# A two-layer token tower: each half of the tokens as one chain, experts group by group, gate rows by DMA

## The reference, cut to what matters

```python
h = embed(tokens, pp)                                 # table rows through one linear map
# layer 0
x = layernorm(h); k, q = tanh(gelu(x@W1+b1)@W2+b2)    # keys and queries, 64 phases each
ret = causal(cos/sin(q) . cos/sin(k)) @ (x@Wv)        # per sequence, divided by position
h = h + x + layernorm(ret)@Wo + bo
h = moe(h, experts=8, top_k=2, hidden=256, gelu)      # operand normalised per expert
# layer 1
x = four blocks of (linear attention, 8 heads; feed forward 64 -> 256 -> 64, gelu)
h = h + ...; h = moe(h, experts=8, top_k=2, hidden=256, relu)
```

## Time and profile before

| what | value |
|---|---|
| median of 3 runs | 662.95 us (662.91 to 663.2) |
| profiled execution | 665.71 us, its span 664.0 us |
| PE busy | 564.1 us (85% of the span) |
| DVE busy | 423.9 us (64%) |
| ACT busy | 405.1 us (61%) |
| granted TensorE clock, mean | 0.928 of full |
| DMA moved | 11.03 MB |

### The profile page before, as it was taken

How to read it: one execution, slowest core, us unless ns; L and a number is a source line. 1 busy time by engine, 2 the same in 40 slices (tenths; PEclk the granted TensorE clock), 3 DMA queues, 4 the chain that set the end, 5 groups by cost and what they waited for, 6 DMA issues and landing times.

```text
span 664.0 us, 8277 instructions
## 1 busy us (share of the span) xinstructions
PE 564.1 (85%) x2840; PEld 294.7 (44%) x2862; DVE 423.9 (64%) x1105; ACT 405.1 (61%) x674; POOL 24.0 (4%) x36
## 2 busy tenths in 40 slices
PE   0679793599899999867999999999864998999995
PEld 0345783434333333355676666766523333333331
DVE  6779579645333453588899999999866254333333
ACT  0458231286576676424978878888741666766773
POOL 8060000000000000000000000000000000000000
PEclk9979796799899999896999999999986899999998
DMA  7901000000000000300000000000000000001001
GB/s 209 219 1 36 13 1 0 1 0 1 0 1 0 1 0 1 95 1 0 1 1 1 1 2 1 0 1 1 1 0 1 0 1 0 1 1 32 1 0 32
DMA packets 16343, 11.03 MB, mean 17 GB/s; under 512 B 10064, under 2 KB 15216, under 8 KB 16240
## 3 DMA queue, kind: packets, MB, share of 16 engines
q1 hardware_dynamic: 14000, 9.93, 6.0%
q10 hardware_dynamic: 2304, 0.58, 0.5%
HBM read 9.47 MB, written 1.05 MB: 16 GB/s over the span
## 4 chain that ended last, share of the span: by engine, by line
PE 54%; DVE 32%; issue 6%; ACT 4%; DMA 3%; SPq 1%; DVEq 0%; ACTq 0%
PE bank L1521 20%; PE bank L1537 18%; DVE l1mom L1204 3%; DVE Xs L1197 3%; DMA w1m<-in_w1e 3%; PE bank L1526 2%; PE bank L1328 2%; DVE Xn L1229 2%; PE bank L1394 2%; DVE mom L831 1%; DVE small L1165 1%; DVE Cen L1210 1%; PE bank L1385 1%; DVE Mm L1190 1%; DVE Ph L1159 1%
## 5 line engine op out<-in xcount | busy, mean ns | idle before, releaser
L652 ACT ACTIVATE Hd<-bank,b1all 128x512 f32<-128x512 f32 x256 | 155.5, 690 | 74.2 <-PE bank L1521 74.2
L1537 PE MATMUL bank<-Hd,w2m 128*64 128x512 f32 x512 | 123.1, 604 | 5.0 <-issue 5.0
L1060 DVE SCALAR_TENSOR_TENSOR Tmp<-bank,b2col,Wb 128x512 f32<-128x512 f32 x56 | 42.0, 751 | 130.6 <-PE bank L1537 130.6
L1521 PE MATMUL bank<-Ph,w1m 64*128 64x512 f32 x256 | 69.0, 644 | 3.6 <-ACT Hd L652 2.1
L1521 PE MATMUL bank<-XT,w1m 64*128 64x512 f32 x256 | 67.6, 638 | 3.9 <-ACT CT L636 1.7
L1537 PEld LDWEIGHTS bank<-Hd,w2m 128*64 128x64 f32 x512 | 31.5, 136 | 52.3 <-issue 51.5
L712 ACT ACTIVATE Hd<-bank,lvecs 128x512 f32<-128x512 f32 x64 | 38.9, 688 | 5.7 <-PE bank L1658 5.5
L1521 PEld LDWEIGHTS bank<-Ph,w1m 64*128 64x128 f32 x256 | 24.8, 193 | 38.6 <-ACT Hd L652 19.3
L1521 PEld LDWEIGHTS bank<-XT,w1m 64*128 64x128 f32 x256 | 23.9, 193 | 40.3 <-ACT Hd L652 21.6
L1064 DVE TENSOR_TENSOR Rest<-Rest,Tmp 128x512 f32<-128x512 f32 x56 | 38.8, 692 | 1.9
L1609 PEld LDWEIGHTS bank<-bd,XT 128*128 128x128 f32 x256 | 32.8, 200 | 16.1 <-ACT Hd L712 15.0
(11 more groups left out here) (220 smaller groups left out, 911.8 us busy)
## 6 DMA issues: line engine op xcount, KB each, us to landing
Ph<-in_x SPq DMA_DIRECT2D x4, 512.0 KB, 9.2
Ph<-in_itok SPq DMA_DIRECT2D x4, 384.0 KB, 9.9
w1m<-in_w1e SPq DMA_DIRECT2D x1, 1028.0 KB, 18.6
w2m<-in_w2e SPq DMA_DIRECT2D x2, 512.0 KB, 13.7
w1m<-in_w1e SPq DMA_DIRECT2D x1, 1024.0 KB, 5.7
out<-Hs SPq DMA_DIRECT2D x16, 64.0 KB, 1.7
Hd<-in_w1all SPq DMA_DIRECT2D x1, 512.0 KB, 14.9
bd<-in_l_attn SPq DMA_DIRECT2D x8, 64.0 KB, 4.6
```

The lines of the kernel that those rows point to most:

```text
L652: ac.activation(Hd[:, st.ring, k // 2, k % 2, :], bank[k][:, :], func, bias=b1all[:, m, st.e, k // 2:k // 2 + 1]).then_inc(up_read, 1)
L1060: ve.scalar_tensor_tensor(dst, bank[4 + st.ring][:, :], b2, Wb[:, st.ring, :], ALU.add, ALU.mult).then_inc(down_read, 1)
L1521: te.matmul(bank[k][:, :], w1m[hs, st.e, k // 2 * P:(k // 2 + 1) * P], operand[hs, gslice(st.g)], start=True, stop=True).then_inc(up_made, 1)
L1537: ins = te.matmul(bank[4 + st.ring][h * D:(h + 1) * D, :], w2m[:, st.e, hc * D:(hc + 1) * D], Hd[:, st.ring, hc, h, :], start=(hc == 0), s ...
```

## The change

The names of bank plan, step order and lists all change, but what is computed stays, except that the phases are reduced by another formula and gates stay float32.

- **Half by half.** PE, ACT and DVE take half 0 through scores, retrieval, norms, projection, operand and gates as early as their lists let them, with pieces of half 1 between. `norm_retrieved(1)` is behind half 0's gates, and half 1's projection, norms and operand run beside the first 16 steps.
- **Phases in two passes** instead of three (scale and offset go into the sine's own scale and bias); ACT's sines stand between gelus and tanhs of other groups.
- **Steps group by group.** Step n has group n // 8 and expert n % 8; each group is turned back and normed while the next ones run. The norm before layer 1 is per group for groups 2 and 3.
- **Gates by transfers.** The 16 gate rows of a group are turned in float32, copied to `CT` (now `[16, 2048]`), written to a DRAM scratch (`spill`), and per step two DMAs from there broadcast one row each over 64 partitions of `Wb` (`spread`), which is now a ring of 4. The `select` matmul, the copy from bank 6 and the three bf16 parts are gone. The DMAs are all in SP's list, with the stores of the output between those of the second MoE.
- **Smaller moves.** `bias_through_w1` goes right behind the embedding; the scaling of `w1m` (8 ACT instructions that waited for a DMA inside the embedding) goes behind the tanhs; a gelu table is loaded before the first step; the hand-over's turns, gate and routing move one beat up.

```diff
 class Step:
-    def __init__(self, m, u, pair, n):
-        self.m, self.n, self.s, self.g = m, n, n // 2, 2 * u + n % 2
+    def __init__(self, m, n):
+        self.m, self.n = m, n
+        self.g, self.e = n // E, n % E
+        self.t = STEPS * m + n
         self.ring = n % 2
+        self.down_bank = 5 - self.ring
...
+            def spill(m, g):
...
+                taken(sp, ("ct", m, g))
+                sp.dma_start(gate_rows[m, g], CT[:, gslice(g)]).then_inc(rows_out[g], 16)
...
+            def spread(st):
...
+                sp.wait_ge(rows_out[st.g], 16 * (st.m + 1))
+                if st.t >= RING:
+                    sp.wait_ge(down_read, st.t - RING + 1)
+                for h in range(2):
+                    sp.dma_start(Wb[h * D:(h + 1) * D, st.t % RING, :],
+                                 gate_rows[st.m, st.g, h * E + st.e].partition_broadcast(D)).then_inc(
+                                     wb_in[st.t % RING], 16)
...
+            def all_gates(m):
+                for n in range(STEPS):
+                    if n % 16 == 0:
+                        for g in (n // E, n // E + 1):
+                            spill(m, g)
+                    spread(Step(m, n))
+                    if m == 1 and n in (15, 22, 30):
+                        store((n - 14) // E)
...
-                step(ve.tensor_scalar(Ph[:, g, :], Ph[:, g, :], turn[:, 0:1], turn[:, 3:4], ALU.mult, ALU.add))
...
-                step(ve.tensor_scalar(Turn[:, :], Ph[:, g, :], ROUND, -ROUND, ALU.add, ALU.add))
...
-                ve.tensor_tensor(Ph[:, g, :], Ph[:, g, :], Turn[:, :], ALU.subtract).then_inc(frac_ready, 1)
...
+                step(ve.tensor_scalar(Turn[:, :], Ph[:, g, :], turn[:, 1:2], turn[:, 2:3], ALU.add, ALU.add))
...
+                ve.scalar_tensor_tensor(Ph[:, g, :], Turn[:, :], turn[:, 2:3], Ph[:, g, :], ALU.subtract,
+                                        ALU.subtract).then_inc(frac_ready, 1)
...
+            phases(0)
+            phases(1)
+            values(0)
...
+            mask_scores(0)
+            values(1)
+            mask_scores(1)
+            phases(2)
+            values(2)
+            norm_retrieved(0)
+            phases(3)
+            attended(0)
+            mask_scores(2)
             attended_in(0)
             layernorm(2, 0, Hs, Xs)
+            operand_norm(0)
+            values(3)
+            mask_scores(3)
+            routed(0, 0)
+            route_weights(0, 0)
             norm_retrieved(1)
+            for n in range(STEPS):
+                weigh(Step(0, n))
+                if n == 4:
+                    attended(1)
+                if n == 5:
+                    attended_in(1)
+                    layernorm(2, 1, Hs, Xs)
+                if n == 6:
+                    operand_norm(1)
+                if n == 10:
+                    mixed(0, 0)
+                    routed(0, 1)
...
+                if n == 18:
+                    mixed(0, 1)
+                    mixed_in(0, 0)
+                    layernorm(4, 0, Hs, Xs)
...
+            experts_in(0)
+            up(Step(0, 0))
+            retrieve(3)
+            for n in range(STEPS):
+                if n + 1 < STEPS:
...
+                    up(Step(0, n + 1))
+                down(Step(0, n))
+                if n == 0:
+                    turn_weights(0, 0)
+                if n == 2:
+                    xt(1, 2, Xn)
+                    xt(1, 3, Xn)
+                if n == 4:
+                    attend0(2)
+                    attend0(3)
...
             for t in range(BEATS):
                 beat(t)
-                if t == JOBS + 1:
+                if t == JOBS:
...
-                    for g in (0, 1):
-                        turn_stream(1, g)
-                    gate(1, 0)
+                    turn_stream(1, 0)
+                    turn_stream(1, 1)
```

More of the change, by code:

```diff
@@ L18 @@
 U = 2
+RING = 4
 GC = 512
@@ L113, in plan_psum, with put, quarters @@
-    moe(0)
-    plan.at["before L1"] = list(plan.count)
-    moe(1)
+    def put(what, *places):
+        for *key, b in places:
+            plan.add((what, *key), b)
+    def quarters(what, g, *banks):
+        for n, b in enumerate(banks):
+            plan.add((what, g, n // 2, n % 2), b)
+    put("table", (0, 2), (1, 3), (2, 4))
+    for g in range(G):
+        put("embed", (g, g % 2))
+        put("rows", (g, 5 + g % 3))
+    put("b1", (0, 6))
+    put("xt", (0, 0, 3), (0, 1, 1))
+    put("enc1", (0, 0, 3), (0, 1, 1), (1, 0, 2), (1, 1, 4))
@@ new lines, in plan_psum @@
+    quarters("score", 2, 2, 1, 0, 2)
+    put("v0", (3, 6))
+    put("ret", (2, 5))
+    quarters("score", 3, 4, 0, 3, 2)
+    put("xm", (0, 0, 7), (0, 1, 1))
+    put("gate", (0, 0, 7))
+    put("xe", (0, 0, 1), (0, 1, 6))
+    plan.at["before experts", 0] = list(plan.count)
+    put("ret", (3, 7))
+    put("ct", (0, 0, 6), (0, 1, 7))
+    put("xt", (1, 2, 6), (1, 3, 7))
+    put("o0", (2, 6), (3, 7))
+    put("xm", (0, 2, 6), (0, 3, 7))
+    put("at", (0, 0, 6))
+    put("gate", (0, 1, 7))
+    put("xe", (0, 2, 6), (0, 3, 7))
@@ L676, in _, with hidden @@
-            prepare(0, 0)
-            experts(0)
+                    key = ("ct", m, g)
+                    full(act, key)
+                    read(ac.copy(CT[:, gslice(g)], ps(key)[0:2 * E, :]), key)
+            def hidden(st):
+                func = ACT.Gelu if st.m == 0 else ACT.Relu
+                for k in range(4):
+                    act.wait_ge(up_made, 4 * st.t + k + 1)
+                    ac.activation(Hd[:, st.ring, k // 2, k % 2, :], bank[k][:, :], func,
+                                  bias=b1all[:, st.m, st.e, k // 2:k // 2 + 1]).then_inc(up_read, 1)
@@ new lines, in down @@
+            def down(st):
+                if not st.first:
+                    pe.wait_ge(down_read, st.t - 1)
+                pe.wait_ge(up_read, 4 * st.t + 4)
+                for hc in range(2):
+                    for h in range(2):
+                        ins = te.matmul(bank[st.down_bank][h * D:(h + 1) * D, :],
+                                        w2m[:, st.e, hc * D:(hc + 1) * D],
+                                        Hd[:, st.ring, hc, h, :], start=(hc == 0), stop=(hc == 1))
+                ins.then_inc(down_made, 1)
@@ L1584, in _ @@
[L1584 to L1591 removed]
+            xt(0, 0, Xs)
+            xt(0, 1, Xs)
+            pe.wait_ge(enc_in, 8 * 16)
+            encode1(0)
+            encode1(1)
+            encode2(0)
+            xt(0, 2, Xs)
+            encode2(1)
+            values(0)
+            values(1)
+            xt(0, 3, Xs)
+            encode1(2)
+            scores(0)
@@ new lines, in _ @@
+            encode2(2)
+            scores(1)
+            retrieve(0)
+            retrieve(1)
+            taken(pe, ("xt", 0, 2))
+            values(2)
+            encode1(3)
+            encode2(3)
+            xt(1, 0, Xn)
+            xt(1, 1, Xn)
+            attend0(0)
+            attend0(1)
+            scores(2)
+            values(3)
+            retrieve(2)
+            scores(3)
+            pe.wait_ge(consts_ready, 1)
+            turn_stream(0, 0)
+            turn_stream(0, 1)
```

662 lines of the change are left out of this document (288 added, 374 removed).

## The result

The changed kernel takes 595.64 us (median of 4, 595.08 to 601.0), the kernel before on the same chip 663.08: ratio 0.900, 95% interval 0.895 to 0.905. I had said 598.

A forecast was written before the change was run, and what follows sets the result against it. PE's list bounds the MoEs, and chains of waits among DVE, ACT and PE bound the stages between. Terms -34.4 - 6.0 - 2.9 - 8.9 - 12.0 - 1.3 = -65.5 us; forecast 598 us, range 582 to 626.

The forecast's parts named there:

- Part 1: Both MoEs: dropping the gate matmul saves PE 0.32 us in each of 64 steps, 20.5 us in all.
- Part 2: MoE steps: gate transfers turn around in 3 to 5 us, costing nothing; DVE inserts fit up to 7.3; 2 us small stalls.
- Part 3: Attention, half 0 walked as a chain: the first up starts at 96 instead of 130.36, 34.4 us earlier.
- Part 4: First MoE: 138.4 us instead of 144.42, -6.0, with half 1's work moved in; first weigh about 17 us after first up.
- Part 5: Layer 1's start: less norm work on DVE shrinks PE's 8.02 us idle; 2.9 us saved, bounds 0 and 8.
- Part 6: Hand-over to the second MoE: earlier turns, gate and routing, no weight copy before up; -8.9 us, bounds 4 and 11.
- Part 7: Second MoE: -12.0 us from shorter steps and no break at half 1's gates; fewer stores at the end, -1.3.
- 1 (relay not shorter): Attention: the relay of DVE, ACT and PE does not shorten, first up at 110 to 115; 612 to 617 us, 14 in 100.
- 2 (VectorE the bound): First 20 MoE steps: DVE becomes the bound, each missed bank about 4 us; three misses give 610 us, 16 in 100.
- 3: Attention's walk: table switches drain ACT, costing 8 us more; 606 us, 5 in 100.
- 4: MoE steps: gates come too late, turnaround 19.6 us makes steps 4.90 us; 669 us, 4 in 100.
- 5: Gains left out: half-clock stretches in the attention vanish, layer 1's start gains 8; 588 us, 10 in 100.

The follow-up runs named there:

- Experiment 1: The changed kernel with GpSimd's removed set-up work (memsets and selects) put back on a spare buffer: 606.14 us, ratio 0.9095.
- Experiment 8: The changed kernel with three hand-over orders: norm's turns after the last feed_up, 595.75 us; previous with VectorE's adds earlier, 598.2; first with earlier add and filler matmuls, 594.69.
- experiments 4: The changed kernel with half 1's attention, projection, norms, turns and operand put back ahead of the first up: 622.15 us, ratio 0.934.
- 7: The changed kernel with half 1's operand_norm moved right behind the norm at step 5, one long VectorE insert: 604.6 us, ratio 0.908.
- experiments 6: The changed kernel with one more activation table load in front of each of the four sines: 604.43 us, ratio 0.9105.
- 3: The changed kernel with one buffer for a step's gates instead of four: 641.57 us in one execution.

## Why the prediction was right

- **Part 1, 0.32 a step:** right. Steps of 3.79; the matmul put back costs 21.3 us against 20.5.
- **Part 2, gates by transfer and inserts:** right. Turnaround 3.57 (3 to 5 said), no `weigh` waits for it after the first two; an insert beyond 7.3 us costs what the sum says, and those of the change lie under it. Of the 2 us for small stalls in each MoE only 0.9 and 0.0 came (TensorE's idle time there): that covers the 1.3 us by which each is shorter than I said.
- **Part 3, the first up:** the walk itself was right to 0.1 us, 27.0 to 96 = 69.0 against 23.35 to 92.49 = 69.1, though single sines took 2.09 instead of 1.84. The 0.1 is partly luck: counted from the first norm, `operand_norm` ended at 66.5 where the walk has 64.9, and shorter masks of group 3 (2.5 instead of 3.1) and the 1 us set aside for the clock took the delay back. Its starting point was wrong by 3.7: I took VectorE's times until the first norm from rows that had been made under GpSimd's work, and that work goes with the change. Experiment 1 put it back and got 3.7 at the first up.
- **Part 4:** right (137.1 against 138.4; first `weigh` 16.96 against 17, `down` 2 0.93 against 0.5).
- **Part 5:** 4.2 instead of 2.9, within its bounds. I did not test it alone.
- **Part 6, the hand-over, was mis-sized:** -6.1 instead of -8.9. From the gelu beat the norm's end was said at 21.6 us and came at 21.7, but I then let turns, gate and the last feed run side by side. They stand in one list on TensorE, so the feed waits 5.67 us for the norm that it does not need. Experiment 8 shortened or moved that wait and brought the first up forward by 1.6 to 7.6 us, though the whole gained nothing clear of noise:

```profile
443.70 1.94 PE L1355 MATMUL bank<-ident,Xn 128*128 128x128 f32 x8 [5.67 <-DVE Xn L935]
...
457.13 1.55 PE L1495 MATMUL bank<-ident,comb 128*16 128x128 f32 x8 [0.93 <-DVE Xs L1233]
...
458.61 5.71 PE L1509 MATMUL bank<-XT,w1m 64*128 64x512 f32 x16
```

Against the earlier trace rows the first up no longer waits for a copy of gates, and the turned weights wait for the last add.
- **Part 7 and the end:** -13.3 against -12.0, -1.3 as said. Of part 7 only the 0.32 a step was tested alone.
- **The rivals:** 1 (relay not shorter) and 2 (VectorE the bound) did not happen, but experiments 4 and 7 brought them about, at 125.4 and at 4.0 us a miss, the price that I had given one. 3 and 4 were refuted by experiments 6 and 3. Of 5, a part was there: the granted clock until the first up rose from 0.84 to 0.98, but layer 1 gained 4.2, not 8. The earlier norm stood in no rival.
- The sum hit 598 closer than its steps deserve: 3.5 us too little at the start, 1.3 too little in each MoE and in layer 1, 2.8 too much at the hand-over, and a clock that adds 0 to 5 from one execution to the next, which the sum has no term for.

## What to carry to other kernels

When a change removes work from an engine that nobody waits for, look at what ran at the same time on the engine beside it: durations read from the old trace may hold the neighbour's share. In a relay of in-order engines list, for each wait, what stands behind it on that engine; a moved wait reappears there (norm, add, tanh), and a walk that runs two chains of one engine side by side comes out too short. A wait of TensorE can cost the clock behind it as well, and whether it does can differ between executions of one program.
